# Causal masks of a decoder's self attention: four products a pass in place of sixteen

## The reference

```
scores = jnp.einsum('bhqd,bhkd->bhqk', q, k) / math.sqrt(Hd)
causal = jnp.triu(jnp.ones((S, S), dtype=bool), k=1)
scores = jnp.where(causal, jnp.finfo(scores.dtype).min, scores)
attn = jax.nn.softmax(scores, axis=-1)
out = jnp.einsum('bhqk,bhkd->bhqd', attn, v)
```

## Time and profile before

| | |
|---|---|
| median of 3 runs | 629.47 us |
| the profiled execution | 630.4 us |
| its span, first to last instruction | 628.5 us |
| instructions in it | 28,714 |
| PE busy | 562.7 us |
| PE weight loads (beside PE) | 435.6 us |
| DVE, ACT, POOL busy | 484.3, 464.3, 425.6 us |
| mean granted clock of TensorE | 0.973 |

### The profile page before, as it was taken

How to read it: one execution, slowest core, us unless ns; L and a number is a source line. 1 busy time by engine, 2 the same in 40 slices (tenths; PEclk the granted TensorE clock), 3 DMA queues, 4 the chain that set the end, 5 groups by cost and what they waited for, 6 DMA issues and landing times.

```text
span 628.5 us, 28714 instructions
## 1 busy us (share of the span) xinstructions
PE 562.7 (90%) x9869; PEld 435.6 (69%) x9869; DVE 484.3 (77%) x1756; ACT 464.3 (74%) x1266; POOL 425.6 (68%) x824
## 2 busy tenths in 40 slices
PE   3798899999999999999999999998847999999994
PEld 2466666666666676666666666666537899999893
DVE  2877888878888878888887887877676877777673
ACT  3765678778677778688786777776426899999893
POOL 3323678888877888878888777878685445554453
PEclk9899999999999999999998999999966999999997
DMA  6511111221111221111211111110012222222210
GB/s 176 66 55 28 29 37 38 70 86 57 54 54 54 69 90 54 55 54 54 90 51 37 38 36 38 47 36 26 11 50 78 66 76 70 72 71 68 66 52 9
DMA packets 55196, 35.59 MB, mean 57 GB/s; under 512 B 14976, under 2 KB 50433, under 8 KB 55056
## 3 DMA queue, kind: packets, MB, share of 16 engines
q1 hardware_dynamic: 50160, 24.44, 14.6%
q0 software_dynamic: 4320, 8.66, 4.1%
q10 hardware_dynamic: 576, 0.66, 0.4%
HBM read 24.46 MB, written 9.74 MB: 54 GB/s over the span
## 4 chain that ended last, share of the span: by engine, by line
PE 78%; issue 8%; ACT 5%; DVE 4%; POOL 2%; SPq 1%; DVEq 1%; DMA 0%; ACTq 0%; POOLq 0%
PE quad L705 9%; PE side L914 8%; PE side L729 6%; PE quad L673 6%; PE quad L903 5%; PE side L790 4%; PE side L903 4%; PE quad L656 4%; PE side L826 3%; PE side L638 3%; PE side L648 3%; PE side L844 3%; PE quad L713 2%; PE side L760 2%; PE side L811 2%
## 5 line engine op out<-in xcount | busy, mean ns | idle before, releaser
L1854 POOL DMA_INDIRECT out<-yo,rb x71 | 69.9, 984 | 70.3 <-issue 38.9
L1015 ACT ACTIVATE prob<-quad 128x1024 f32<-128x1024 f32 x64 | 62.1, 1022 | 41.3 <-PE quad L713 41.3
L992 ACT ACTIVATE ex<-qk,cf 128x512 f32<-128x512 f32 x128 | 85.3, 718 | 0.0
L1818 POOL DMA_INDIRECT expert_rows<-pay,sli x64 | 65.6, 1025 | 21.2 <-issue 16.8
L914 PE MATMUL side<-w,hT 128*128 x568 | 76.7, 278 | 3.5 <-DVE hT L1459 2.9
L1317 DVE TENSOR_REDUCE mx<-quad 128x16 f32<-128x1024 f32 x64 | 74.9, 1213 | 5.8 <-PE quad L673 5.1
L914 PEld LDWEIGHTS side<-w,hT 128*128 128x128 f32 x568 | 69.9, 194 | 4.6 <-issue 4.6
L705 PE MATMUL quad<-ex,qk 32*64 32x256 f32 x1024 | 61.8, 389 | 6.1 <-issue 3.9
L1377 DVE TENSOR_TENSOR y<-side,xn 128x304 f32<-128x304 f32 x32 | 15.2, 474 | 45.7 <-PE side L844 45.0
L705 PEld LDWEIGHTS quad<-ex,qk 32*64 32x64 f32 x1024 | 28.1, 130 | 30.5 <-issue 25.1
L729 PE MATMUL side<-prob,vau 128*32 128x64 f32 x2048 | 42.5, 225 | 2.5 <-ACT prob L1015 2.1
(11 more groups left out here) (242 smaller groups left out, 1689.5 us busy)
## 6 DMA issues: line engine op xcount, KB each, us to landing
rb<-expert_rows SPq DMA_DIRECT2D x71, 68.0 KB
xin<-in_x SPq DMA_DIRECT2D x32, 128.0 KB, 2.8
cin<-in_ctx SPq DMA_DIRECT2D x32, 128.0 KB, 3.0
xr<-in_x SPq DMA_DIRECT2D x32, 128.0 KB
w<-in_w1t SPq DMA_DIRECT2D x8, 256.0 KB, 3.5
w<-in_w2t SPq DMA_DIRECT2D x8, 256.0 KB, 3.3
out<-yo,rb POOLq DMA_INDIRECT x71
expert_rows<-pay,sli POOLq DMA_INDIRECT x64
```

Of the source, the lines that this page charges most:

```text
L992: act(ex[g.par][:, i, :, :].rearrange("p a t -> p (a t)"), qk[g.par][:, :, :].rearrange("p a t -> p (a t)"), ACT.Copy, scale=own4[:, i:i + ...
L1015: act(prob[g.par][:, 2 * h_:2 * h_ + 2, :], quad[:, 2 * h_:2 * h_ + 2, :], ACT.Exp).then_inc(*ac_a.done(f"e{h_}"))
L1818: v.indirect_dma_start(out=rows, out_offset=bass.IndirectOffsetOnAxis(ap=sli[g.par][:, j:j + 1], axis=0), in_=pay[g.par][:, j, :], in_offs ...
L1854: v.indirect_dma_start(out=o_rows, out_offset=bass.IndirectOffsetOnAxis(ap=number, axis=0), in_=yo[b.c % 4][:, :], in_offset=None, bounds_ ...
```

## The change

Each bank takes its mask in one product of 64 rows by 128 columns in place of four of 32 by 32. Banks 0 and 2 use rows 0 to 63 of the tables, banks 1 and 3 rows 64 to 127. The weights are a new table `ii`, the identity of 64 written twice side by side, made by DVE in two casts; the mask tables shrink to 64 columns, since both halves hold the whole 64 by 64 mask. ACT makes each by one copy, and POOL's four fills go. The score products, the maxima and all waits stay as they are.

```diff
-        mask_q = sb("mask_q", [P, 3 * SQ], BF16)
-        mask_k = sb("mask_k", [P, 3 * SQ], BF16)
+        mask_q = sb("mask_q", [P, SQ], BF16)
+        mask_k = sb("mask_k", [P, SQ], BF16)
+        ii = sb("ii", [P, 2, SQ], BF16)
...
             def masked(r_, mask_):
 
-                strip = slice(32 * r_, 32 * r_ + 32)
-                for c in range(4):
-                    mm(quad[32 * c:32 * c + 32, r_, :], ident_b[strip, strip],
-                       mask_[strip, SQ * (c % 2):SQ * (c % 2) + SQ].unsqueeze(1).broadcast_to((32, 512 // SQ, SQ)),
-                       start=True, stop=False, tile_position=(32 * r_, 32 * c))
+                half_ = slice(64 * (r_ % 2), 64 * (r_ % 2) + 64)
+                mm(quad[:, r_, :], ii[half_, :, :].rearrange("p b k -> p (b k)"),
+                   mask_[half_, :].unsqueeze(1).broadcast_to((64, 512 // SQ, SQ)), start=True, stop=False,
+                   tile_position=(64 * (r_ % 2), 0))
...
                 for to, from_ in ((mask_q, nqf), (mask_k, nkf)):
-                    for c in range(4):
-                        at = slice(32 * c, 32 * c + 32)
-                        last = cp(to[at, :].rearrange("p (b c) -> p b c", b=2)[:, :, 0:32],
-                                  from_[at, 32 * (c % 2):32 * (c % 2) + 32].unsqueeze(1).broadcast_to((32, 2, 32)))
+                    last = cp(to[:, :], from_[:, :])
                 last.then_inc(s_masks, 1)
...
                 v.tensor_copy(ident_b[:, :], identf)
+                for c in range(2):
+                    rows_ = slice(64 * c, 64 * c + 64)
+                    v.tensor_copy(ii[rows_, :, :], identf[rows_, rows_].unsqueeze(1).broadcast_to((64, 2, SQ)))
...
-            v.memset(mask_q[:, 32:SQ], NEG)
-            v.memset(mask_q[:, SQ:SQ + 32], 0.0)
-            v.memset(mask_k[:, 32:SQ], 0.0)
-            v.memset(mask_k[:, SQ:SQ + 32], NEG)
```

## The result

The kernel became faster, by 0.7%, where 1.4% slower was forecast. The median is 625.42 us (622.21 to 628.04, nine executions) against 629.07 for the kernel before beside it (628.33 to 631.24, nine); the ratio is 0.9931 (0.9906 to 0.9956). The profiled execution has a span of 623.8 us, 4.7 less than before.

What follows compares the result with a forecast made beforehand. PE was taken to bound the kernel, so longer mask passes lengthen it: 5.7 (`mask_k`) + 4.0 (`mask_q`) - 0.7 (setup) = +9.0 us, 638.5 on the median. Bounds alone gave 637.8 to 644.7; the range 632 to 645.5 held 82%.

Steps and rivals of the forecast that it cites:

- Pairing and the pass: Mask products on PE (L656): two run at once on the array's halves, a pass taking 0.611 us.
- the rival of 0.88 us: Mask pass: third load waits for the first product's end, +26 us, 655.4; 9% together with halves running one after another.
- the working on L811: Sixteen 64 by 64 products in 0.46 us: four rounds of 0.06, so halves run side by side; otherwise 0.69 us.
- `mask_q`, +4.0: 32 mask passes before the maxima's scores: 19.6 less 15.4 us, +4.2, with 0.18 of the first pass hidden.
- `mask_k`, +5.7: 32 mask passes before the exponentials' scores: 32 x 0.611 = 19.6, less 13.9 us.
- the first rival: Score passes beside a scatter: POOL's second start sets their end, growth free in 28 passes; +4.0 us, 633.5; 10%.
- Their number costs next to nothing: Mask pass on PE: sixteen instructions start within 0.05 us, so the sum has no saving for twelve fewer.
- The third rival, instruction supply: Stretched score passes end when 160 instructions have trickled in; 24 fewer save 0.49 us in 28 passes: -9.7, 619.8; 6%.
- Its sign, a stretch below 3.2 us: Instruction supply would show as a stretch from masks to L837 below 3.2 us.
- The setup, -0.7: ACT's eight mask copies become two, so `ex`, and with it L673, starts about 0.7 us sooner.
- the bound of 0: Setup: no gain in place of -0.7 us, if a later load holds the same place.
- The sum: `mask_k` 5.7 + `mask_q` 4.0 - setup 0.7 = +9.0 us: 639.4 against the profiled execution, 638.5 on the median.

Runs made afterwards that it cites:

- series A: Chips where the result and the first four experiments were measured; the kernel before takes 629 to 630 us there.
- series B: Three chips of the later runs; kernel before 596 to 597 us. Unchanged on one of them: before 597.45 us, changed kernel 596.04.
- the shift by 40: Changed kernel with 20 idle products (40 instructions with their loads) on TensorE ahead of everything: 597.90 us; the changed kernel beside it 596.63.
- the split kernel: Changed kernel with each of its four mask products cut by columns into four of 128, sixteen a pass: 631.44 us, 1.0023 of the kernel before.

## Why the prediction was wrong

**Pairing and the pass: right.** The four products start at 0, 0.003, 0.226 and 0.230 us in the trace, and the next line 0.535 after the first; the forecast had 0.213 for the third and 0.54. The union is 19.6 / 32 = 0.613 us for `mask_q` and 19.4 / 32 = 0.606 for `mask_k`, forecast 0.611. The record of the third load, in the rows of the first product, starts 0.011 us after that product and not behind its end, so the rival of 0.88 us falls. By the rule of the Trainium skill, "TensorE: Matmul & The Clock Gate", section The mechanism, it would have waited; these starts disagree with it. (In the working on L811, four rounds of starts have three intervals between them and not four: (0.46 - 0.23) / 3 = 0.08 us each, and eight rounds would take 0.77. The reading stays.)

**`mask_q`, +4.0: right in size.** Unstalled rounds grew by 0.12 to 0.17 us, 3.7 in the 27. What was missed is beside it: 1.8 us in series A and 6.3 in series B came back as single stalls that the shorter program mostly has no longer. That is luck of the place as much as a merit of the change, as the shift by 40 shows.

**`mask_k`, +5.7: wrong, and this is the step that failed.** The prediction put it so: "a pass that takes longer on PE takes the kernel longer; no other engine covers it." In the early passes that held (1.78 to 1.81 us before, 1.95 after), and once the scatter was moved away from the passes (1.78 and 1.95 on the median). In the stalled ones nothing of the array's time reached the end (3.07 and 3.08 us with 19.9 and 13.9 us of it), as the first rival had it, and the pass became shorter besides, by 0.14 us on the median and 4.8 us in 27. The argument against that rival, "a later start leaves more of them", had the right idea and the wrong sign. What is left when the stall ends depends on how many products PE had issued by its last stop, a number that is nearly the same in both kernels, and with twelve fewer ahead of them the score products are further on.

**"Their number costs next to nothing": wrong where PE is held up by issue.** The third rival, instruction supply, had the direction. It priced 24 instructions at 0.49 us a stalled pass; the split kernel against the changed one measures 0.11 on the median and 0.15 on the mean. Its figure came from dividing the whole pass by its instructions, where only the part behind the stop counts. Its sign, a stretch below 3.2 us, was also set by one pass of 3.27; the kernel before has 3.11 on the median, so the sign would have shown in most of its own passes. By the estimate from the Trainium skill, "TensorEngine Tiling (Array Packing)", section Instruction Overhead, 0.3 us a pass would be saved in all 64; series B shows no such saving, its passes became longer by 0.05 and 0.12 us.

**The setup, -0.7: the bound of 0 was right.** ACT's exponentials did start sooner, but L673 began only 0.1 us sooner and the first `mask_k` pass 0.07. Three lines of after, and then L673 of before and of after:

```profile
17.45 2.56 ACT L989 ACTIVATE ex<-qk,cf 128x512 f32<-128x512 f32 x4 [0.71 <-POOL qk L1723]
...
26.80 0.29 PE L686 MATMUL side<-ident_b,mt 128*32 128x128 bf16 x8 [0.92 <-ACT mt L999]
27.60 0.60 PE L656 MATMUL quad<-mask_k,ii 64*128 64x512 bf16 x4 [0.51 <-DVE vau L1224]
...
20.94 2.01 PE L673 MATMUL quad<-ex,qk 32*64 32x256 f32 x32 [1.17 <-ACT ex L992]
20.84 1.12 PE L673 MATMUL quad<-ex,qk 32*64 32x256 f32 x32
```

`ex` begins at 17.45 (forecast 17.6, before 18.32), and the first `mask_k` pass at 27.60, where it was 27.67. The two executions can't be compared closely here, since the clock ran another course: before it was 0.51 from 20.8 to 24.2 us, where L673 took 2.01 us, and after PE's products have the lengths of the lower level until 20.5, ahead of the first row that the trace has on the clock (the group of L649 at 18.97 takes 1.20 us, that of L648 before 0.69). In the pair of series B the first such row is at 20.0 and 20.1 us, and there L673 begins 0.35 us sooner (21.13 and 20.78) and the first `mask_k` pass no sooner at all (27.81 and 27.86): the two waits in the lines above, for `mt` and for `vau`, take back what was won.

**The sum.** In series A: the maxima stretch +1.9 (+3.7 less 1.8 of single stalls), the score passes -4.8, the rest -1.5 (the clock of the execution before), together -4.4 us. The forecast had +9.7 for the two kinds of pass together. The difference is 10.5 us in the score passes and 2.1 in the maxima stretches, both about how PE is fed, where the prediction looked at the array only, and 1.5 of clock, which is no part of the change.

**What stays open.** Why a scatter start of POOL stops PE for 1.2 us in series A and hardly in series B was not found, nor whether the chip is what makes the difference. In series B `mask_k` cost 0.05 us a pass in place of 0.17: the passes of before vary from 1.78 to 2.08 us there, with POOL's second start in them, and take 1.78 on the median where the scatter is moved away; those of after take 1.95 in both. So the scatter seems to cost the passes of before some 0.13 us here too, in a way that was not found. What a stall of the block's end waits for in the 2.2 us since its packet began, and what makes that packet late, was not tried either.

## What to carry to other kernels

Where the profile calls a wait "issue", read which instruction stands behind it and how many are left of its stage; there fewer instructions gained here, even with more work in each, while in a stretch without such waits the array's time counted. So choose the form of each pass by its own stretch: here pairs for the one beside the scatter and 32 by 32 tiles for the other gave 0.9883. Where the stall is missing the same kernel gave 0.9963, but through fewer single stalls; its score passes cost 2 us there. Count the instructions of a loop's round against the block of 256: a change of a few dozen can move single stalls in or out, and such a gain or loss belongs to the place and not to the edit. And before a stretch of a trace is compared with another, look at the granted clock of both: one fall for 3.4 us was 1.5 of the 4.4 us here.

## What the runs showed of the hardware

- One kernel took 629 to 630 us in series A and 596 to 597 on the three chips of series B, 5.5%. Score passes that run beside an indirect scatter make the difference (3.11 and 1.91 us on the median, 33 us in 27); the other two parts of the round had the same medians to 1 ns.
- PE stopped for 0.4 to 1.4 us at one place of a 256 instruction block (record 193) in 18 maxima stretches, 17 times in products of 32 by 64 and once in those of 32 by 32, and never sooner than 2.2 us after the start of a packet of its instruction queue. 40 instructions more ahead of everything moved the stops to other rounds.
- The granted clock fell to 0.50 for 3.4 us in single places of an execution (341.7 us in that of the kernel before); L811 took 0.64 us there in place of 0.46, and the round 1.5 us more.
- Products of 64 rows by 128 columns on the two halves of the array run side by side, and the next pair starts 0.226 us behind, in the same rows, 0.16 us before the modelled end of the first; its loads start 0.011 us after the first.
